# Output projection of the last two batches moved into the token-choice block, their router logits made from the product of both weights

## The chip, the cores and the metric

The kernel runs on one core of a Trainium2 chip. The metric is the time of one execution on the device, in microseconds (us).

## The reference, cut to what matters

Sixteen batches of 256 tokens with 256 features pass through a conditioned feed-forward layer (first block), then through a layer with attention of 16 heads of 64 and a mixture of 8 experts. What matters here is the end of attention and the choice of tokens:

```python
o = o.transpose(0, 2, 1, 3).reshape(b, n, H * HD)      # (tokens, 1024)
x = x + o @ Wout.T                                     # the output projection
tok = x.reshape(-1, d)                                 # 4096 x 256
gate = _softmax(tok @ Wgate.T, axis=-1)                # router logits, 8 experts
vals, idx = jax.lax.top_k(gate.T, k_cap)               # 512 tokens for each expert
...
g = _ln(tok[idx_flat], mlp_g, mlp_b)                   # gathered rows, normalised
...
tok = tok.at[idx_flat].add(y.reshape(-1, d))
```

## The kernel before

The program is three blocks with a barrier between them: `first_block`, `attention` and, in `experts`, a routing block followed by the expert block. Each engine has its own queue of instructions, written out in a fixed order, and waits on semaphores. An fp32 product is made of three products of high and low parts (`product`, line 147), so one 128-row tile of the output projection is 8 x 3 = 24 matmuls of 128x128 on 128x256.

**Attention** is one pipeline over steps t from -2 to 17, each of 8 head pairs s. In pair s of batch t TensorE does the scores of the pair (L1103), the transposes of the pair before (L1115) and the values of an older pair (L1130). VectorE takes the lowest score of each row (L1487), ScalarE the exponentials (L1258), and the scores of the next pair may start only when the exponentials have emptied the score banks. GpSimd divides (L1386). Into this pattern are put: parts of the next batches' q, k, v (`chunk`), "fills" on bank `tr` (`fill_at`: `h`, `qk`, and for the batch two steps back `x2`, the transposes of its new rows, L1201, and `gates`, its logits, L1206), and in pairs 2 and 3 the output projection of the batch before (`project`).

The last batch, 15, has no step after it. Its projection is done by head pair as `project_last` (L1154) in pairs 4 to 7 of step 15 and in `finish`; then VectorE adds the residual rows (`x2`, L1511), TensorE transposes them, ScalarE copies them, TensorE makes the logits and ScalarE puts them into `logit` (L1289). SyncE stores the new rows to `out` and the normalised rows to `x2_rows`.

**Routing.** After the barrier SyncE loads five small tables and then 8 MB of expert weights already split in halves (`load_halves`). VectorE and ScalarE make the softmax; TensorE transposes the gates (L1662). Then the 512th largest gate of every expert is found in 15 rounds ("digits"): VectorE counts against two trial values, ScalarE against a third with `Sign` (L1654), TensorE adds the counts (L1671), VectorE makes the next trial. TensorE fills the time with `idle_products` of the identity matrix (L1585), which nobody reads.

**Expert block.** GpSimd gathers rows from `x2_rows` by indirect DMA (L1971), TensorE transposes them (L1909), then two products for each expert, and GpSimd adds the results to `out`.

At the head of attention (t = -2 and -1) there are no scores yet. VectorE must first normalise the rows of batch 1, which SyncE loads after the barrier.

## Time and profile before

| what | value |
|---|---|
| median of 3 runs | 1431.27 us (1431.09 to 1432.25) |
| the profiled execution, time | 1431.61 us |
| its span, first to last instruction | 1429.8 us |
| TensorE busy | 1370.5 us, 96% |
| mean granted TensorE clock | 0.987 |

The profile lists each instruction or group with its start, duration, engine, source line and tiles ("out<-in"); in brackets stands the idle time ahead of it and what ended it. A TensorE row's duration overlaps the next row's: rates are read from the distance of starts. Granted clock 1.0 is 2.4 GHz, 0.5 is 1.2 GHz.

### The profile page before, as it was taken

What the parts mean: (1) busy time and instruction counts of PE and PEld (TensorE: products, weight loads), DVE (VectorE), ACT (ScalarE), POOL (GpSimd) and SP (SyncE); (2) the same over time, 40 slices, a digit from 0 to 9 for tenths busy, and PEclk for the clock granted to TensorE, in tenths of its full rate; (3) what the DMA queues carried; (4) which work ended last, traced back from release to release, by engine and by line L of the source; (5) the groups of instructions that cost most, each with busy time, mean ns of one, the idle gap of its engine ahead of it and who ended that gap; (6) DMA issues with size and microseconds to landing.
All of it is one profiled execution on the core that took longest, in us unless ns stands there. A gap on an engine that the chain in (4) does not pass through costs nothing. (4 is left out here: it accounts for less than half of the span.)

```text
span 1429.8 us, 30429 instructions
## 1 busy us (share of the span) xinstructions
PE 1370.5 (96%) x10795; PEld 1183.3 (83%) x10795; DVE 960.7 (67%) x2191; ACT 1035.9 (72%) x2703; POOL 911.5 (64%) x855
## 2 busy tenths in 40 slices
PE   7899999997899999999999999999999988999996
PEld 6799999996678887888888788788888777889896
DVE  5876667643776676677667667666755568678763
ACT  5556666565898889889888988988988732476662
POOL 2576666652678768867877876786787620354643
PEclk9899999999999999999999999999999999999999
DMA  5342222111100100110110011011011046145522
GB/s 159 114 129 67 68 67 68 49 45 30 38 9 30 53 23 31 53 45 9 52 46 31 30 53 36 18 53 45 9 45 46 30 148 253 45 104 156 137 35 30
DMA packets 61638, 89.04 MB, mean 62 GB/s; under 512 B 6144, under 2 KB 50992, under 8 KB 58800
## 3 DMA queue, kind: packets, MB, share of 16 engines
q1 hardware_dynamic: 53232, 75.82, 16.3%
q0 software_dynamic: 6144, 8.39, 3.6%
q10 hardware_dynamic: 2112, 2.88, 0.6%
q8 instruction: 87, 1.43, 0.4%
q14 instruction: 63, 0.52, 0.1%
HBM read 61.90 MB, written 25.18 MB: 61 GB/s over the span
## 5 line engine op out<-in xcount | busy, mean ns | idle before, releaser
L1386 POOL TENSOR_TENSOR prob<-prob,share_p 128x512 f32<-128x512 f32 x256 | 271.6, 1067 | 195.6 <-DVE share_p L1493 195.0
L1487 DVE TENSOR_REDUCE shift<-bank 128x2 f32<-128x512 f32 x256 | 164.7, 685 | 186.0 <-PE bank L1103 185.9
L1258 ACT ACTIVATE prob<-bank,shift 128x256 f32<-128x256 f32 x512 | 237.8, 479 | 64.3 <-DVE shift L1487 64.2
L147 PE MATMUL bank<-wqkv_h,rowsT_h 128*128 128x512 f32 x384 | 158.9, 414 | 2.8 <-PEq L311 1.7
L147 PE MATMUL bank<-wqkv_h,rowsT_l 128*128 128x512 f32 x384 | 151.5, 395 | 0.0
L147 PE MATMUL bank<-wqkv_l,rowsT_h 128*128 128x512 f32 x384 | 150.8, 393 | 0.0
L1115 PE MATMUL bank<-ident,prob 128*128 128x128 f32 x1024 | 142.7, 281 | 1.1 <-POOL prob L1386 1.1
L1374 POOL TENSOR_TENSOR landing<-landing,rq 128x512 f32<-128x512 f32 x128 | 131.1, 1046 | 8.4 <-DVE rq L1441 8.4
L1130 PE MATMUL bank<-pT,landing 128*64 128x256 f32 x1024 | 127.1, 388 | 1.7 <-ACT pT L1345 1.7
L1115 PEld LDWEIGHTS bank<-ident,prob 128*128 128x128 f32 x1024 | 109.5, 141 | 21.3 <-POOL prob L1386 3.7
L1258 ACT ACTIVATION_READ_ACCUMULATOR prob<-bank,shift 128x1 f32 x512 | 107.5, 210 | 0.0
L640 POOL TENSOR_TENSOR hid_l<-hid,hid_h 128x512 fp32r<-128x512 f32 x64 | 86.1, 1355 | 30.7 <-ACT hid_h L536 30.0
L1282 ACT ACTIVATE landing<-bank,cols 128x512 f32<-128x512 f32 x128 | 101.9, 796 | 4.9 <-PE bank L1196 3.3
L532 ACT ACTIVATE hid<-bank,cols 128x256 f32<-128x256 f32 x128 | 53.3, 470 | 68.0 <-PE bank L147 68.0
L1130 PEld LDWEIGHTS bank<-pT,landing 128*64 128x64 f32 x1024 | 67.5, 137 | 41.3 <-issue 9.8
L1103 PE MATMUL bank<-kT_h,qT_h 64*128 64x256 f32 x512 | 85.5, 329 | 2.7 <-ACT prob L1258 2.7
L1518 DVE COPY pT<-bank 128x512 f32<-128x512 f32 x128 | 87.2, 681 | 0.2 <-PE bank L1115 0.2
L1302 ACT ACTIVATE landing<-bank 128x512 f32<-128x512 f32 x128 | 80.2, 627 | 9.2 <-PE bank L147 9.1
L1483 DVE TENSOR_REDUCE ssq<-raw_sq 128x8 f32<-128x512 f32 x128 | 85.8, 673 | 1.3 <-ACT raw_sq L1304 0.8
L147 PEld LDWEIGHTS bank<-wqkv_h,rowsT_h 128*128 128x128 f32 x384 | 72.8, 190 | 16.3 <-issue 2.4
L1196 PE MATMUL bank<-ident,landing 128*128 128x128 f32 x512 | 78.2, 276 | 7.9 <-ACT landing L1282 3.7
L147 PEld LDWEIGHTS bank<-wqkv_h,rowsT_l 128*128 128x128 f32 x384 | 72.5, 189 | 15.8
(324 smaller groups left out, 4517.6 us busy)
## 6 DMA issues: line engine op xcount, KB each, us to landing
landing<-in_fc1s SPq DMA_DIRECT2D x6, 1024.0 KB
landing<-in_fc2s SPq DMA_DIRECT2D x6, 1024.0 KB
rows<-in_x SPq DMA_DIRECT2D x16, 256.0 KB, 2.9
xT<-in_xT SPq DMA_DIRECT2D x16, 256.0 KB, 2.7
x_again<-in_x SPq DMA_DIRECT2D x16, 256.0 KB, 2.8
x_rows<-x SPq DMA_DIRECT2D x16, 256.0 KB, 3.1
rows<-x_rows SPq DMA_DIRECT2D x16, 256.0 KB, 3.1
x<-x_rows SPq DMA_DIRECT2D x16, 256.0 KB, 2.9
```

The source lines that it names most:

```text
L147: last = nc.tensor.matmul(out, a, b, start=(n == 0), stop=(n == 3 * len(ks) - 1))
L640: nc.gpsimd.tensor_tensor(hid_l[:, 2 * g:2 * g + 2, :], hid[:, 2 * g:2 * g + 2, :], hid_h[:, 2 * g:2 * g + 2, :].bitcast(F32), ALU.subtrac ...
L1103: mm = nc.tensor.matmul(score_bank[side][:, n * T:(n + 1) * T], q[r, at, n * P:(n + 1) * P], k[r, at, :], start=(i == 0), stop=(i == 2))
L1115: last = nc.tensor.transpose(pT_bank[side][:, m * T + n * P:m * T + (n + 1) * P], prob[q % 2 * 2 + side][:, n, m * P:(m + 1) * P], ident[: ...
L1130: last = nc.tensor.matmul(values_bank(b, q)[side * HD:(side + 1) * HD, :], v[its][:, m, h * HD:(h + 1) * HD], pT[q % 2 * 2 + side][:, m, : ...
L1258: last = nc.scalar.activation(prob[at][:, n, :], score_bank[side][:, n * T:(n + 1) * T], ACT.Exp, bias=shift[:, at, n:n + 1], scale=-1.0, ...
L1282: nc.scalar.activation(raw_block(j), tr[:, :].rearrange("p (m n) -> p m n", m=4), ACT.Identity, bias=cols[:, g + 1:g + 2], scale=cols[:, g ...
L1374: nc.gpsimd.tensor_tensor(part, part, rq[:, n, c * 8:(c + 1) * 8].unsqueeze(2).to_broadcast([P, 8, HD]), ALU.mult).then_inc(normed, 1)
L1386: nc.gpsimd.tensor_tensor(prob[at][:, :, :], prob[at][:, :, :], share[:, at, :].unsqueeze(2).to_broadcast([P, TT, T]), ALU.mult).then_inc( ...
L1483: nc.vector.tensor_reduce(ssq[:, n, c * 8:(c + 1) * 8], raw_sq[c % 2][:, :].rearrange("p (h d) -> p h d", h=8), AX, ALU.add).then_inc(summ ...
L1487: nc.vector.tensor_reduce(shift[:, s % 2 * 2 + side, :], score_bank[side][:, :].rearrange("p (n m) -> p n m", n=TT), AX, ALU.min).then_inc ...
L1518: nc.vector.tensor_copy(pT[q % 2 * 2 + 1][:, :, :].rearrange("p m n -> p (m n)"), pT_bank[1][:, :]).then_inc(pT_dve, 1)
```

## The change

For the last `LATE` = 2 batches (14 and 15) attention no longer makes the projection. A matrix `wc`, Wgate times Wout (1024 x 8, in a high and a low part side by side, 16 columns), is made once at t = -1. `logits_of` multiplies it with the high and low parts of `o`: 16 matmuls with 256 moving columns for a batch. ScalarE copies the 16x256 result (`from_o`), and the `gates` fill adds it to the logits of the residual rows by one more small matmul for each 128 rows. The `x2` fill now transposes the residual rows themselves. `CLOSING_FILLS` says where these fills go.

The projection of both batches is done in the routing block: eight steps of three matmuls before the transposes of the gates, two steps in each of rounds 0 to 11 in place of the idle products. The rows of the batch are added by a matmul of the identity on `late_x`. ScalarE takes the result out, sums and squares it and normalises it between its `Sign` instructions, GpSimd makes the root. `o` of batch 14 is kept in DRAM meanwhile (`keep_o`), and is loaded into the place of the second early expert's first weights, which are loaded later.

The rows of batch 1 are loaded by SyncE in the last step of the first block. Buffers of `o`, `wout` and others share room with those of other blocks, and `ew_raw` becomes `ew_l`, so the next piece is loaded only when the store of the one before has landed.

```diff
+CLOSING_FILLS = {(NB - 1, 9): (NB - 2, "x2"), (NB - 1, 11): (NB - 2, "gates"), (NB - 1, 13): (NB - 1, "x2"), (NB, 3): (NB - 1, "gates")}
+LATE_PAIR = {False: PROJ_PAIRS[0], True: PROJ_PAIRS[1]}
...
@@ first_block, SyncE
+                    if at(t, NB):
+                        sp.wait_ge(tr_h, 1)
+                        sp.wait_ge(x1_out, 32)
+                        sp.dma_start(x_t[:, :, :], x1_rows[T:2 * T, :].rearrange("(t p) d -> p t d", p=P)).then_inc(x1_in, 16)
...
@@ attention, SyncE
+                    if t == -1:
+                        for q in range(4):
+                            sp.dma_start(prob[q][:, :, :], a["woutT"][:, q * T:(q + 1) * T].rearrange("(k p) n -> p k n", p=P)).then_inc(wc_in, 16)
...
+                    if is_late(t - 1) and live(t):
+                        keep_o(t - 1, (0, 2, 4, 6))
...
@@ attention, TensorE
+                def logit_weights():
+                    pe.wait_ge(wc_in, WC_IN + 64)
+                    for m in range(PAIRS):
+                        for k in range(KT):
+                            last = nc.tensor.matmul(score_bank[0][:, m * E:(m + 1) * E], prob[m // 2][:, k, m % 2 * P:(m % 2 + 1) * P], wgate[:, k, :],
+                                                    start=(k == 0), stop=(k == KT - 1))
+                    last.then_inc(wc_made, 1)
...
-                def project_last(k, its):
...
+                def logits_of(b, half, its):
+                    wait(pe, o_lo, PAIRS, b, 4 * half + 4)
...
+                    for k in range(4 * half, 4 * half + 4):
+                        for n, part in enumerate((o_h, o_l)):
+                            last = nc.tensor.matmul(chunk_bank[0][0:2 * E, 0:T], wc[:, k, :], part[:, o_at(k, its), :],
+                                                    start=(k == 0 and n == 0), stop=(k == PAIRS - 1 and n == 1))
...
                 def finish(t, its):
-                    fill(t, 1)
                     values(t - 1, PAIRS - 2, its)
                     transposes(t - 1, PAIRS - 1)
-                    project_last(PAIRS - 3, its)
+                    logits_of(t - 1, 0, its)
+                    values(t - 1, PAIRS - 1, its)
+                    logits_of(t - 1, 1, its)
                     fill(t, 3)
-                    values(t - 1, PAIRS - 1, its)
-                    project_last(PAIRS - 2, its)
-                    project_last(PAIRS - 1, its)
...
+                        if t == -1 and s == 2:
+                            logit_weights()
...
-                        if closing(t) and s in PROJ_PAIRS:
-                            project(t - 1, PROJ_PAIRS.index(s), 1 - odd)
-                        if closing(t) and s >= 4:
-                            for k in range(0 if s == 4 else s - 3, s - 2):
-                                project_last(k, odd)
                         if closing(t):
+                            if s == LATE_PAIR[True]:
+                                logits_of(t - 1, 0, 1 - odd)
+                                logits_of(t - 1, 1, 1 - odd)
                             fill(t, 2 * s + 1)
...
@@ routing block
+LATE_STEPS = [2] * 12 + [0] * 3
+TAKEN_IN, SPREAD_IN, NORMED_IN = {4: 1, 8: 2, 12: 3}, {5: 1, 9: 2, 13: 3}, {1: 0, 7: 1, 11: 2}
...
@@ routing, SyncE (after the five tables)
+                    for i, b in enumerate(LATE_ORDER):
+                        sp.dma_start(late_x[i][:, :, :], x1_rows[bass.ds(b * T, T), :].rearrange("(t p) d -> p t d", p=P)).then_inc(late_in[i], 16)
+                        if i > 0:
+                            load_late_o(i)
+                    load_halves(sp, w1_in, (w1_h, w1_l), halves[0:2], 0)
                     for e in range(EARLY):
-                        load_halves(sp, w1_in, (w1_h, w1_l), halves[0:2], e)
                         load_halves(sp, w2_in, (w2_h, w2_l), halves[2:4], e)
...
+                    for i, b in enumerate(LATE_ORDER):
+                        if i > 0:
+                            sp.wait_ge(late_made, NB + TT * (i + 1))
+                            load_halves(sp, w1_in, (w1_h, w1_l), halves[0:2], 1)
+                        sp.wait_ge(late_normed, NB + TT * (i + 1))
+                        for rows, tile, last in ((x2_rows, late_n[i], last_rows), (out, late_x[i], last_out)):
...
@@ routing, ScalarE
                     nc.scalar.activation(gates[:, :, :], gates[:, :, :], ACT.Exp).then_inc(exped, 1)
+                    take(0)
+                    spread_of(0)
                     for n in range(DIGITS):
...
@@ routing, TensorE
-                    idle_products(6)
+                    def late_step(i, k):
...
+                        if k == 0 and i % TT == 0 and j > 0:
+                            pe.wait_ge(late_in[j], 16 + 48)
+                        if k == HW // P - 1 and i == 0:
+                            pe.wait_ge(late_in[0], 16 + 16)
...
+                        for m, (o, w) in enumerate(((high, wo_h), (high, wo_l), (low, wo_h))):
+                            nc.tensor.matmul(late_bank(i), o[:, k, rows], w[:, k, :], start=(k == 0 and m == 0), stop=False)
+                        if k == HW // P - 1:
+                            nc.tensor.matmul(late_bank(i), ident[:, :], late_x[j][:, i % TT, :], start=False, stop=True).then_inc(late_made, 1)
+
+                    for k in range(HW // P):
+                        late_step(0, k)
+                    done = HW // P
                     pe.wait_ge(gated, 1)
...
-                    idle_products(6)
                     for n in range(DIGITS):
...
-                        idle_products(6)
+                        for _ in range(LATE_STEPS[n]):
+                            late_step(done // (HW // P), done % (HW // P))
+                            done += 1
+                        if LATE_STEPS[n] == 0:
+                            idle_products(6, 2, 384)
...
@@ expert block, GpSimd
+                        if first(later):
+                            pool.wait_ge(last_rows, 16 * (LATE_FROM + 1))
```

## Rows read from the trace of the kernel before

**Rows 1.** The page, busy time and share of TensorE.
```profile
PE 1370.5 (96%) x10795; PEld 1183.3 (83%) x10795; DVE 960.7 (67%) x2191; ACT 1035.9 (72%) x2703; POOL 911.5 (64%) x855
```

**Rows 2.** Timeline of TensorE, step 15: start us, us; scores, then one projection tile.
```profile
1126.44 0.39 PE L1103 MATMUL bank<-kT_h,qT_h 64*128 64x256 f32 x2
...
1132.44 0.38 PE L1103 MATMUL bank<-kT_h,qT_h 64*128 64x256 f32 x2
...
1135.39 0.39 PE L147 MATMUL bank<-wout_h,o_h 128*128 128x256 f32 x1
...
1138.24 0.28 PE L147 MATMUL bank<-wout_h,o_l 128*128 128x256 f32 x1
...
1150.71 0.39 PE L1103 MATMUL bank<-kT_h,qT_h 64*128 64x256 f32 x2
```

**Rows 3.** Timeline of TensorE, the tail after the last scores.
```profile
1155.04 1.08 PE L1130 MATMUL bank<-pT,landing 128*64 128x256 f32 x8
...
1156.90 0.36 PE L1154 MATMUL bank<-wout_h,o_h 128*128 128x256 f32 x1
...
1158.93 1.08 PE L1130 MATMUL bank<-pT,landing 128*64 128x256 f32 x8
...
1160.96 0.38 PE L1154 MATMUL bank<-wout_h,o_h 128*128 128x256 f32 x1
...
1164.97 1.03 PE L1206 MATMUL bank<-wgate,proj 128*128 128x8 f32 x8 [0.78 <-ACT proj L1286]
```

**Rows 4.** Timeline of ScalarE and VectorE in the same stretch.
```profile
1129.90 0.21 ACT L1258 ACTIVATION_READ_ACCUMULATOR prob<-bank,shift 128x1 f32 x1
...
1162.72 0.76 DVE L1511 TENSOR_TENSOR x<-bank,x 128x256 f32<-128x256 f32 x2 [1.82 <-DMA x<-x_rows]
...
1166.04 0.18 ACT L1289 ACTIVATE logit<-bank 128x16 f32<-128x16 f32 x1 [1.21 <-PE bank L1206]
```

**Rows 5.** Timeline of SyncE's queue in the routing block.
```profile
1167.08 0.35 SPq L1635 DMA_DIRECT2D tables<-in_tables  x1
...
1169.45 0.36 SPq L1589 DMA_DIRECT2D ew_h<-split_w1h  x1
...
1195.50 0.33 SPq L1595 DMA_DIRECT2D landing<-in_fc2s  x1
```

**Rows 6.** The tile `x_rows`: from issue to landing, all its transfers.
```profile
DMA to landing us min/median/max: 2.1/3.0/5.3
```

**Rows 7.** Timeline of the routing block: gates, first and last round.
```profile
1170.21 0.44 PE L1662 MATMUL bank<-ident,gates 128*128 128x128 f32 x2 [0.18 <-DVE gates L1713]
...
1171.54 0.51 ACT L1654 ACTIVATE signs<-key,trial 128x256 bf16<-128x256 f32 x1 [2.68 <-DVE key L1720]
...
1198.96 0.51 ACT L1654 ACTIVATE signs<-key,trial 128x256 bf16<-128x256 f32 x1 [1.30 <-DVE trial L1764]
```

**Rows 8.** Groups by line: a squaring pass of ScalarE with a sum.
```profile
L540 ACT ACTIVATE junk_act<-rows 128x256 f32<-128x256 f32 x32 | 12.9, 405 | 1.5 <-DMA rows<-in_x 1.5
```

**Rows 9.** Timeline at the head of attention.
```profile
330.62 0.75 DVE L1446 BATCH_NORM_STATS2 stats<-rows 128x6 f32<-128x256 f32 x2 [3.60 <-DMA rows<-x_rows]
...
334.68 0.50 PE L147 MATMUL bank<-wqkv_h,rowsT_h 128*128 128x512 f32 x1 [0.82 <-ACT raw_sq L1304]
...
341.55 0.66 PE L1196 MATMUL bank<-ident,landing 128*128 128x128 f32 x4 [0.63 <-POOL landing L1374]
...
342.97 0.81 ACT L1282 ACTIVATE landing<-bank,cols 128x512 f32<-128x512 f32 x1
```

**Rows 10.** Window 1218:1220 us: busy by engine, PEclk, DMA share, GB/s.
```profile
1218.00:1220.00 2.00, 1.00 (x12) 0.55 (x11) 0.00 (x0) 0.00 (x0) 1.04 (x2) 0.50 0.22 70
```

**Rows 11.** Timeline of the expert block's start: the same small matmul twice, the first gather.
```profile
1211.35 0.29 PE L1902 MATMUL bank<-rec,spread 128*128 128x48 f32 x1 [0.33 <-DVE rec L2022]
...
1212.98 2.14 POOL L1971 DMA_INDIRECT gx<-x_rows,next_index  x1 [0.18 <-POOL idle L1958]
...
1220.40 0.41 PE L1902 MATMUL bank<-rec,spread 128*128 128x48 f32 x1 [0.30 <-DVE rec L2022]
```

More of the change, by code:

```diff
@@ L926, in fill_at, with attention @@
             slot += 1
-        if slot == i:
+        if slot == i and not (name in ("x2", "gates") and t + TR_LAG[name] >= NB - 2):
             return t + TR_LAG[name], name, j
     return -1, None, 0
-def attention(nc, exponent, weights, rows_of, banks, ident, x1_rows, hbias, cols, x2_rows, logit, out, a, halves, sbuf, sems):
+def attention(nc, exponent, weights, rows_of, banks, ident, x1_rows, hbias, cols, x2_rows, logit, out, a, halves, out_weights, o_kept, o_stored,
+              spent, sbuf, sems):
+    wo_h, wo_l, o_h, o_l, _ = out_weights
+    wc_in, wc_made, wc_done = spent
     landing, o_raw, wgate, wo_hi, wo_lo, (x2_stored, x2n_stored, ew_stored) = weights
@@ L1543, in step @@
                             chains(t, i + 1, spot)
+                        if t == -1 and s == 2:
+                            logit_weights()
                         for j in range(8):
@@ L1558, in _, with experts @@
                 steps(step)
-def experts(nc, a, landing, halves, banks, ident, cols, x2_rows, logit, out, stored, sbuf, sems):
+LATE_STEPS = [2] * 12 + [0] * 3
+TAKEN_IN, SPREAD_IN, NORMED_IN = {4: 1, 8: 2, 12: 3}, {5: 1, 9: 2, 13: 3}, {1: 0, 7: 1, 11: 2}
+def experts(nc, a, exponent, landing, halves, banks, ident, cols, x1_rows, x2_rows, logit, out, stored, out_weights, o_kept, o_stored,
+            spent, sbuf, sems):
+    late_stored, late_made, late_taken, late_centred, late_squared, late_normed, late_rooted, late_links, *late_in = spent
+    wo_h, wo_l, o_h, o_l, kept = out_weights
     s = ExitStack()
@@ new lines, in _ @@
+                    sp.wait_ge(late_stored, LATE_STORED + 32 * (LATE - 1))
+                @block.gpsimd
+                def _(pool):
+                    link = Links(pool, late_links)
+                    link.base = NB
+                    for i in range(LATE * TT):
+                        one = slice(i, i + 1)
+                        pool.wait_ge(late_squared, NB + i + 1)
+                        link(nc.gpsimd.tensor_scalar(late_var[:, one], late_sq[:, one], 1.0 / D, LN_EPS, ALU.mult, ALU.add))
+                        link(nc.gpsimd.tensor_tensor(late_root[:, one], late_var[:, one], exponent[:, :], ALU.pow))
+                        nc.gpsimd.tensor_tensor(late_shift[:, one], late_mean[:, one], late_root[:, one], ALU.mult).then_inc(late_rooted, 1)
```

271 lines of the change are left out of this document (177 added, 94 removed).

## The prediction

> **What bounds the kernel now.** I read the page first: TensorE is busy for 96% of the span [rows 1], so a matmul taken away counts where TensorE is what ends last, and nowhere else. The last step of attention and the routing block are the places touched, so I read their timelines next, engine by engine.
>
> In step 15 a head pair without additions is 2.95 us of TensorE work (scores 1132.44, first projection matmul 1135.39). A projection tile adds 24 matmuls between 1135.39 and 1138.24, which is 0.12 us each and about 3.06 us with the change of operands: pair 2 lasts 6.00 us [rows 2]. But there is a second loop under it. The last exponential of pair 2 is read out at 1129.90 + 0.21 = 1130.11, 3.67 us after its scores began [rows 2, 4], and the next scores may not start before. So a pair can't be shorter than about 3.75 us, however little TensorE has to do. The reader is to see that 0.8 us of each bare pair is not TensorE's.
>
> After the last scores the tail is a chain: values of pair 7 at 1158.93, the last part of the projection at 1160.96, the new rows on VectorE only at 1162.72 because their residual came by a late DMA, logits at 1164.97, `logit` written at 1166.04 [rows 3, 4]. The routing block starts at 1167.08 [rows 5]. In it the chain is gates transposed (1170.21), first `Sign` (1171.54), and 14 steps of (1198.96 - 1171.54) / 14 = 1.96 us to the last one [rows 7]. TensorE's idle products there cost nothing: this stretch is a chain through all engines, and it is where the moved work goes.
>
> **The change part by part: steps 15 and 16.** I move through it with the starts before as clock.
> - Pair 2 loses its tile and falls on the floor: 3.75 for 6.00 us, -2.25.
> - Pairs 3 to 6 took 1150.71 - 1132.44 = 18.27 us [rows 2]. After: pair 3 with 16 matmuls of `logits_of`, 2.95 + 16 x 0.12 + 0.2 = 5.05; pair 4 with the `x2` fill, four transposes at 0.23, 3.87; pair 5 with the `gates` fill, 8 small matmuls in 1.03 [rows 3] and two more of the same kind, 0.25, 4.2; pair 6 with the other `x2` fill, 3.87. Sum 16.99, -1.28. That a 16-column stationary tile streams like one of 128 is my assumption; the moving side has the same 256 columns.
> - Pair 7 to the values of pair 6: 4.33 us before (1155.04), bound by ScalarE's copy of the transposed tile after the exponentials; 4.2 after, -0.13.
> - From 1155.04 the values and transposes are as before until 1156.90 [rows 3]; then 8 matmuls of `logits_of` (1.15 us, to 1158.05) for the work that held the values of pair 7 back to 1158.93: -0.88. Running sum -4.5.
> - The tail: values to the last projection part was 1160.96 - 1158.93 = 2.03. After it: 8 matmuls and their latency 1.1, ScalarE's copy of 16x256 with its semaphores 0.5, the gates fill 1.07 to the start of the `logit` copy [rows 3, 4] plus 0.25. The `logit` copy starts 2.03 + 1.1 + 0.5 + 1.32 = 4.95 us after the values; before it was 1166.04 - 1158.93 = 7.11: -2.16. The late residual DMA, its add, the transposes and the copy leave the path.
>
> Sum -6.7. If pair lengths are 0.15 over my floor and the small copies cost 0.5 more it is -5.9; if the barrier, which last followed SyncE's store, comes faster, -7.3.
>
> SyncE is moved past too: the eight stores of `keep_o`, the 2 waits for landing in `load_piece`, the residual loads of batches 14 and 15. They are issued pairs before their readers; batch 14's rows are wanted only at the end of pair 4. Covered, 0; without the cover each would cost its landing, median 3.0 [rows 6].
>
> **Routing: what waits first.** Eight late steps are put ahead of the gate transposes on TensorE. 21 of their matmuls run at once, but the last three wait for `late_x[0]`, which SyncE issues after the five tables. The sixth transfer of this block was issued at 1169.45 [rows 5]; a read or write of `x_rows` lands 3.0 us after issue in the median, 2.1 at least, 5.3 at most [rows 6]. So the rows are there at 1172.45, and behind them in TensorE's order stand three matmuls (0.46 with the start), the identity matmul on 256 fp32 columns (0.24, twice a 128-column one) and then the transposes of the gates, at about 1173.2 for 1170.21 [rows 7]: +3.0. ScalarE has `take(0)` and `spread_of(0)` ahead of its first `Sign`: 0.41 each [rows 8], 0.2 each for reading the sum [rows 4] and a small one between, some 1.4 us from 1173.3, to 1174.7. VectorE has the key at 1174.5. `Sign` is thus 0.2 late, and VectorE's two counts, longer, hide it. I take +3.0; bounds by the landings +2.1 and +5.3.
>
> In the rounds two late steps are 6 x 0.12 = 0.7 us against a round of 1.96, after the sum of counts and not ahead of it; 0. ScalarE's extra passes (at most 1.4 us behind a `Sign` of 0.7) leave nothing over in rounds 5, 9 and 13 but do fit by about 0.2; a miss costs a few tenths. GpSimd is free here. `o` of batch 14 is wanted in round 4, some 8 us after the first; fine.
>
> **Head of attention.** VectorE no longer waits 3.60 us for the rows of batch 1 [rows 9]; its sums then come earlier and TensorE's wait of 0.82 goes. But `logit_weights` puts 16 small matmuls, twice the 1.03 us of the gates fill [rows 3], at the place where TensorE idled 0.63 before the first `qk` fill at 341.55 [rows 9]. After: last chunk ends 0.9 earlier, 2.0 us of these, fill at 342.05. ScalarE empties the fill at 342.97, held by its own queue [rows 9]; that queue is up to 0.9 ahead, the fill's data 0.5 late and ready at 342.7: -0.2 in all. Bounds: -0.9 (all of the early rows) and +0.6 (none of it, the products in full).
>
> **Sum.** -6.7 + 3.0 - 0.2 = -3.9. The profiled execution took 1431.61, 0.34 over the median, at 1429.8 of span; I apply the difference to the median: 1431.27 - 3.9 = 1427.4 us.
>
> **The rivals.** (1) *The full gain*, if the rows of batch 15 are not waited for: 24 matmuls from 1167.13 end at 1170.0, when the gates are ready anyway. Then +0.2 for +3.0: 1424.6. The three last matmuls would want the rows at 1169.7, with an issue at 1169.45 [rows 5]; rows 6 show no landing under 2.1. So it is left only as a landing at the minimum together with more from the tail or the head: 0.07.
>
> (2) *The clock.* TensorE now stands about 3 us before the gates and has 6 matmuls for 12 idle products in a round. Where it had stood about half of the time, the clock granted was 0.50 [rows 10], and the same small matmul took 0.41 for 0.29 us [rows 11]. If the rounds run at 1.2 GHz, each has 0.12 more on its chain: 15 x 0.12 = +1.8, 1429.2. Against it: 6 x 256 columns are as many as 12 x 128. 0.15. The Trainium skill ("TensorE: Matmul & The Clock Gate", "HAM oscillation") has the same warning, that gaps between bursts of matmuls bring the lower clock back; it speaks against taking the filler out, and by it the sum would be rival 2's. Rows 10 agree that a sparse stretch loses the clock; whether this one does, none shows.
>
> (3) *Slower: the gather waits for rows.* GpSimd's first gather (1212.98 before, about 1216 by the clock above) now waits until batch 14's `x2_rows` have landed. They are stored after the last late norm, near 1203, behind the second fc2 megabyte (issued 1195.50 before [rows 5]), the b2 rows, and 2 MB of `w1` halves. At 9 MB in the 26 us from 1169.45 to 1195.50 these 4.5 MB take 13 us, to about 1210. It decides from 1216 on; the kernel is slower by 0.2% only with a landing 6.8 us later still, 1223. Price at 1225: +9 - 3.9 = +5, 1436. 0.07.
>
> (4) *The pairs don't shrink*: the gain of steps 15 and 16 is only that of the tail, -3.0, and the sum is 0: 1431.2. Speaks for it: five engines share the loop. Against: TensorE's rows are back to back there. 0.05.
>
> **How the numbers follow.** The forecast has 0.66. Within 0.2% is +-2.9 us, about what a measurement can tell. The forecast's own range is 1425.5 to 1429.2 (tail -7.3 to -5.9, landing, head). The range 1424.0 to 1430.2 takes in rivals 1 and 2. Faster by over 0.2%, below 1428.4: most of the forecast (0.58), rival 1 (0.07), a third of rival 2 (0.05): 0.70. Slower: rival 3 and overruns of landings, 0.08. The rest, 0.22, is the same.
>
> **What would show it.** Right: step 15's scores at pair 3 start 3.75 us after those of pair 2; the `logit` copy of batch 15 near 1159.4 and the barrier near 1160.4; TensorE then idle for some 3 us up to a DMA wait, the gates transposed 6.1 us after the block's first DMA (3.1 before); 15 rounds of 1.96. Wrong: a gate transposition at 3.3 us (rival 1), PEclk of 0.5 in the rounds (2), an idle GpSimd before the first gather with a DMA as releaser (3), pairs of 5 us (4). I would also be wrong if a 16-column product streamed slower, or the sums on ScalarE stretched rounds 5, 9 and 13.

## The result and the profile after

| | median, us | lowest to highest | profiled execution, its span | mean granted clock |
|---|---|---|---|---|
| before | 1431.12 | 1429.31 to 1434.29 (20 runs) | 1431.61, 1429.8 | 0.987 |
| after | 1432.99 | 1430.89 to 1438.23 (20 runs) | 1433.03, 1431.2 | 0.981 |

The ratio after to before is 1.0019, 95% interval 1.0012 to 1.0026: 1.9 us slower (0.13%), inside the 0.2% that I called the same, and 5.6 us above the forecast of 1427.4. The range of 1424.0 to 1430.2 doesn't hold it.

The two profiles differ by 1.4 us, measured to the start of the last matmul. Cut at events that both have, the difference lies here (from the timelines; B is the routing block's first instruction on TensorE):

| stretch | before | after | difference | predicted |
|---|---|---|---|---|
| start to attention's first matmul | 328.00 | 328.17 | +0.2 | 0 |
| to the first `logit` copy (head) | 145.57 | 147.55 | +2.0 | -0.2 |
| to the 13th `logit` copy (12 full steps) | 609.21 | 610.06 | +0.9 | 0 |
| to B (steps 15 and 16) | 84.35 | 78.29 | -6.1 | -6.7 |
| B to the first `Sign` | 4.41 | 8.65 | +4.2 | +3.0 |
| first to last `Sign` | 27.42 | 28.68 | +1.3 | 0 |
| to the last matmul | 219.79 | 218.71 | -1.1 | 0 |
| sum | | | +1.4 | -3.9 |

So most of the gain is there (how much of it is the change's own is worked out in the section on why the prediction was wrong), and five other stretches together cost more than it. TensorE's row of the page, for [rows 1], gives no hint of that; it is 3.7 us less busy in a longer span:

```profile
PE 1366.8 (95%) x10707; PEld 1177.7 (82%) x10707; DVE 956.1 (67%) x2178; ACT 1043.8 (73%) x2727; POOL 913.2 (64%) x864
```

**Step 15** (answers to [rows 2]). Timeline of TensorE, first scores of pairs 2 to 7:

```profile
1128.84 0.39 PE L1147 MATMUL bank<-kT_h,qT_h 64*128 64x256 f32 x2
...
1132.56 0.38 PE L1147 MATMUL bank<-kT_h,qT_h 64*128 64x256 f32 x2 [0.71 <-ACT prob L1306]
...
1138.20 0.39 PE L1147 MATMUL bank<-kT_h,qT_h 64*128 64x256 f32 x2
...
1141.93 0.39 PE L1147 MATMUL bank<-kT_h,qT_h 64*128 64x256 f32 x2
...
1146.65 0.39 PE L1147 MATMUL bank<-kT_h,qT_h 64*128 64x256 f32 x2
...
1150.38 0.39 PE L1147 MATMUL bank<-kT_h,qT_h 64*128 64x256 f32 x2
```

Pair 2 is 3.72 us, and TensorE stands 0.71 there for the last exponential: the floor that I had worked out at 3.75. The pair with a `x2` fill is 3.73 (3.87 predicted). The pair with the additions of `logits_of` is 5.64 (5.05), the one with the `gates` fill 4.72 (4.2). Pairs 3 to 6 together are 17.82 us, for 16.99 predicted and 18.27 before.

The tail (answers to [rows 3, 4]), timeline of TensorE and ScalarE:

```profile
1159.59 1.11 PE L1196 MATMUL bank<-kept,wc 128*16 128x256 f32 x8 [0.94 <-DVE kept L1575]
...
1163.58 0.18 ACT L1339 ACTIVATE logit<-bank 128x16 f32<-128x16 f32 x1 [2.42 <-PE bank L1254]
```

The values of pair 7 start at 1157.56, so the `logit` copy follows them by 6.02 us: 4.95 was predicted, 7.11 was before.

The 16-column product streams like a 128-column one (8 records in 1.11 us), so that assumption held.

**Head of attention** (answers to [rows 9]), timeline of TensorE, then ScalarE:

```profile
339.86 3.97 PE L1130 MATMUL bank<-wgate,prob 128*128 128x8 f32 x32
343.68 1.09 PE L1241 MATMUL bank<-ident,landing 128*128 128x128 f32 x4
...
344.82 0.78 ACT L1330 ACTIVATE landing<-bank,cols 128x512 f32<-128x512 f32 x1 [2.60 <-PE bank L1241]
```

`logit_weights` is 16 matmuls in the code, and 32 records and 3.97 us in the trace. I had priced it at 2.0, from the fill of [rows 3], whose "x8" are the records of 4 matmuls and not 8 matmuls. ScalarE, which had been behind [rows 9], now waits 2.60 us for TensorE.

**Routing** (answers to [rows 5, 7]), timeline of TensorE, SyncE and ScalarE:

```profile
1164.08 4.82 PE L1814 MATMUL bank<-kept 128*128 128x256 f32 x21 [0.53 <-PEq L1064]
1164.15 0.33 SPq L1726 DMA_DIRECT2D tables<-in_tables  x1
...
1167.55 0.43 SPq L1732 DMA_DIRECT2D late_x<-x_rows  x1
...
1170.39 0.62 PE L1814 MATMUL bank<-kept 128*128 128x256 f32 x3 [1.49 <-DMA late_x<-x_rows]
...
1171.28 0.38 PE L1823 MATMUL bank<-ident,gates 128*128 128x128 f32 x2
...
1172.73 0.49 ACT L1792 ACTIVATE signs<-key,trial 128x256 bf16<-128x256 f32 x1
...
1174.30 1.63 PE L1814 MATMUL bank<-kept 128*128 128x256 f32 x6
```

The order is the predicted one: 21 late matmuls, a stand for the rows of batch 15, three more, the identity, the gates, and ScalarE's `take` and `spread_of` before the first `Sign`. Two things are not. The rows are issued 3.4 us after the block's first transfer (2.4 assumed; one table's issue took 1.56). And the 21 matmuls took 4.82 us, 0.23 each where the same kind takes 0.12 in [rows 2]: in 1164:1168 the granted clock is 0.50, half of it. Six such matmuls in a round took 1.63 us, and with the count sum before them they fill 2.0 us, so that TensorE sets the pace. The rounds of the two kernels, from one `Sign` to the next (us):

| | 1 | 2 | 3 | 4 | 5 | 6 | 7 | 8 | 9 | 10 | 11 | 12 | 13 | 14 |
|---|---|---|---|---|---|---|---|---|---|---|---|---|---|---|
| before | 2.15 | 1.90 | 1.90 | 1.90 | 1.90 | 1.91 | 2.42 | 1.90 | 1.90 | 1.91 | 1.90 | 1.90 | 1.90 | 1.90 |
| after | 2.18 | 2.01 | 2.00 | 2.00 | 2.59 | 1.93 | 2.42 | 1.90 | 2.12 | 1.93 | 1.90 | 1.90 | 1.90 | 1.90 |

Windows over the rounds, before and after (us, then busy time and instructions of TensorE, its weight loads, VectorE, ScalarE, GpSimd; granted clock; DMA share and GB/s):

```profile
1172.00:1180.00 8.00, 7.15 (x56) 6.58 (x57) 7.01 (x39) 2.55 (x10) 0.00 (x0) 1.00 1.01 423
1180.00:1188.00 8.00, 7.18 (x57) 6.42 (x56) 6.90 (x42) 2.27 (x9) 0.00 (x0) 1.00 1.01 418
```

```profile
1172.00:1180.00 8.00, 6.36 (x26) 5.70 (x26) 6.77 (x35) 3.57 (x12) 0.93 (x3) 0.53 1.00 407
1180.00:1188.00 8.00, 6.13 (x34) 5.34 (x34) 6.30 (x37) 3.12 (x12) 0.94 (x3) 0.83 1.01 426
1188.00:1196.00 8.00, 6.45 (x34) 5.53 (x34) 6.75 (x37) 4.20 (x15) 0.92 (x3) 0.79 0.77 317
```

The sixth number, after POOL's, is the granted clock: 1.00 before, 0.53, 0.83 and 0.79 after. The busy times look alike, because at half the clock the same work keeps TensorE busy for longer; the instruction counts are the thing to read, 56 against 26 in the first window. At the full clock six late matmuls are 0.96 us of TensorE, and the 12 records of idle products that they replace were 1.58.

### The profile page after: what moved, and what is told of

Read it like the earlier page. It is cut to its first block and busy times, and to the rows that moved or that the text cites. A ratio compares the mean times of both kernels' runs of the same rounds, so it can differ in the third digit from the quotient of the medians.

```text
span 1431.2 us, 30291 instructions
## 1 busy us (share of the span) xinstructions
PE 1366.8 (95%) x10707; PEld 1177.7 (82%) x10707; DVE 956.1 (67%) x2178; ACT 1043.8 (73%) x2727; POOL 913.2 (64%) x864
## 5 line engine op out<-in xcount | busy, mean ns | idle before, releaser
L147 PE MATMUL bank<-kept 128*128 128x256 f32 x1440 | 183.1, 285 | 0.0
L147 PEld LDWEIGHTS bank<-kept 128*128 128x128 f32 x1440 | 175.3, 191 | 0.0
L656 POOL TENSOR_TENSOR kept<-hid,kept 128x512 fp32r<-128x512 f32 x64 | 86.4, 1360 | 31.1 <-ACT kept L552 30.5
L147 PE MATMUL bank<-kept,w_h 128*128 128x256 f32 x512 | 95.8, 287 | 0.0
L147 PE MATMUL bank<-ew_h,kept 128*128 128x256 f32 x512 | 94.2, 283 | 0.0
```

Source lines behind the costliest of these rows:

```text
L147: last = nc.tensor.matmul(out, a, b, start=(n == 0), stop=(n == 3 * len(ks) - 1))
L656: nc.gpsimd.tensor_tensor(hid_l[:, 2 * g:2 * g + 2, :], hid[:, 2 * g:2 * g + 2, :], hid_h[:, 2 * g:2 * g + 2, :].bitcast(F32), ALU.subtrac ...
```

## The experiments

Each is made from the changed kernel unless said otherwise. The kernel before ran beside them on the same chip (medians 1430.9 for the first four, 1431.1 for the next four, 1430.88 for the three after and 1432.58 for the last), and ratios are to it. In code cuts `...` stands for lines left out.

### The head, the late rows, the idle products

**One eighth of the products of wc.**

```diff
-                    for m in range(PAIRS):
+                    for m in range(1):
```

> Of the eight groups of wc = wo x wg in the head only the first is made (2 of its 16 matmuls), and its result is copied into all eight, so the logits of the last two batches are not the reference's; nothing else is left out. Theory (the products lie on the path: 32 records, 3.97 us, in the changed kernel's trace, and everything behind stands about 2.1 us later): the kernel is 1.7 to 2.3 us faster than the changed one, near 1430.9, and the first qk fill of the head starts near 341.6 instead of 343.7. Rival (the head is late because the clock granted there is 0.50, and the products only fill a gap): less than 0.5 us, 1432.6 to 1433.0. Second rival (the products cost, but ScalarE's queue holds the next wait, as I reckoned before): 0.5 to 1 us.

Measured: 1433.82 us, ratio 1.0018 (1.0010 to 1.0027).

**Products of wc in four lots.**

```diff
+                        if t == -1 and s in (4, 5, 6):
+                            logit_weights(range(2 * s - 6, 2 * s - 4))
                         fill(t, 2 * s)
...
-                        if t == -1 and s == 2:
-                            logit_weights()
+                        if t == -1 and s == 3:
+                            logit_weights(range(0, 2))
```

> All products of wc are made, but in four lots of 4 matmuls ahead of four qk fills (in pairs 3 to 6 of the head) instead of 16 in one place. Theory (the cost of the 16 is that they stand together where TensorE has no slack, and where there is slack later, as TensorE waits for a bank behind ScalarE, a lot of 1 us hides): 1 to 2 us faster than the changed kernel, 1431 to 1432. Rival (TensorE sets the pace of every pair of the head, so work is work): no difference, 1432.7 to 1433.3.

Measured: 1431.31 us, ratio 1.0001 (0.9992 to 1.0009). By whole times this is a contradiction: taking the products away gains nothing, spreading them 1.7 us. The stages settle it. From the last `Sign` on, the run with one eighth takes 221.0 us for 218.7; its logits choose other tokens, so that its whole time can't be compared. And the head depends on the clock it happens to be granted. All profiled executions of the study, head (attention's first matmul to the first `logit` copy) against the mean granted clock in 340:400:

| kernel | 0.94 | 0.91 | 0.89 |
|---|---|---|---|
| before, and before with fewer idle products | 145.57 | 147.25 | |
| products in one place (after and four variants) | 145.85, 145.90, 145.92 | 147.51, 147.55 | |
| one eighth of the products | | 146.35 | |
| four lots (five variants) | 144.67, 144.69 | 146.10, 146.25, 146.45 | |
| products in one place, batch 1's rows late | | | 149.84 |

Within a column each kind lies within 0.35 us. One step of the clock costs 1.65 us, whatever the kernel. At the same clock the changed head costs +0.3 over before, the 16 products in one place 1.2 over none, and in four lots they cost nothing. What is left against before, -0.9 in one column and -1.0 in the other, I put down to the early load; the direct test of it further down did not settle it. So the theory on the products holds, at 1.2 us and not at 2 (read from one execution with one eighth of them and from five with the four lots); of the profile's +2.0 us, 1.7 was the clock that this execution was granted.

**Rows of batch 15 ahead of the tables.**

```diff
+                    sp.dma_start(late_x[0][:, :, :], x1_rows[...]).then_inc(late_in[0], 16)
                     for t, src in ((tables[:, :], a["tables"]), ...
```

> SyncE issues the load of batch 15's rows before the five tables of the routing block and not behind them. Theory (the start of the routing block is bound by the landing of these rows, issued 3.4 us after the first of the block's transfers): they land 3 us sooner, the gates are transposed about 1.5 us sooner (then the 21 matmuls of the late steps at half clock, ending 4.8 us after the block's first, are next), the kernel 1 to 2 us faster, 1431 to 1432. Rival (the late matmuls at half clock bind already, and the landing is hidden): under 0.3 us. Second rival (the tables, then late, become what the first Sign waits for): no gain or a loss of up to 1 us, with a wait of ScalarE or VectorE for a DMA.

Measured: 1432.23 us, ratio 1.0009 (1.0001 to 1.0018). Timeline of TensorE, its late matmuls and the gates:

```profile
1163.59 3.78 PE L1815 MATMUL bank<-kept 128*128 128x256 f32 x21 [0.53 <-PEq L1064]
1168.23 1.01 PE L1815 MATMUL bank<-kept 128*128 128x256 f32 x3 [0.85 <-DMA late_x<-x_rows]
1169.03 1.05 PE L1817 MATMUL bank<-late_x,ident 128*128 128x256 f32 x2
1169.88 0.63 PE L1824 MATMUL bank<-ident,gates 128*128 128x128 f32 x2
```

The gates come 6.29 us after B for 7.20, less than the 1.5 expected, since TensorE still gets the rows 4.6 us after their issue at 1163.66 and the matmuls behind them run at half clock. B to the first `Sign` is 7.82 for 8.65. The rounds took 30.86 us in this execution, with the clock between 0.50 and 0.67 in three windows of 8 us: the small gain of the start can be lost in them.

**Six idle products back behind the gates.** Their line (`idle_products(6, 2, 384)`) was put back where the kernel before has it.

> The changed kernel with the six products on idle operands put back behind the transposes of the gates, where the kernel before had them. Theory (the clock of 0.50 in the first rounds comes from the 2 us in which TensorE then has nothing, and at it six late matmuls take 1.63 us, so that rounds last 2.0 to 2.6 us instead of 1.9): the granted clock rises sooner, first to last Sign takes 27.4 to 27.9 for 28.68 us, the kernel 0.7 to 1.2 us faster, 1431.8 to 1432.3. Rival (the low clock comes from the stand before the rows land, and six products more cannot mend it): within 0.3 us, and the rounds keep 28.7. Second rival (the products stand ahead of the count sum and delay it): slower by up to 0.7 us.

Measured: 1433.42 us, ratio 1.0020 (1.0009 to 1.0030): no gain. Windows over the rounds:

```profile
1172.00:1180.00 8.00, 5.25 (x37) 4.34 (x35) 7.00 (x37) 3.19 (x11) 0.93 (x3) 1.00 1.00 412
1180.00:1188.00 8.00, 5.62 (x31) 4.63 (x30) 6.80 (x42) 3.81 (x15) 0.94 (x3) 0.80 1.01 424
```

They only move the fall: the clock is 1.00 in the first rounds, which hold 5.25 us of TensorE in 8, and then falls inside the rounds, where nothing had been put back. First to last `Sign` is 28.18 us. That the fall came from the missing six alone, which was my theory, is refuted. All twelve runs lie between 1431.3 and 1438.9 us with mean clocks of 0.985 down to 0.974, the longest at the lowest.

### What decides the clock in the rounds

**Idle products in each round**, beside those behind the gates:

```diff
-                        if LATE_STEPS[n] == 0:
-                            idle_products(6, 2, 384)
+                        idle_products(6 if LATE_STEPS[n] == 0 else 3, 2, 384)
```

> The changed kernel with three products on idle operands in each round that has late steps (six more records, some 0.75 us of TensorE at 2.4 GHz, behind the six late matmuls) and six behind the transposes of the gates. Theory (a late step's six matmuls take 0.96 us at the high clock where the kernel before had 12 records of idle products in 1.58 us; TensorE is then busy 1.2 to 1.35 us in each 2 us instead of 1.93, the granted clock falls to 0.50, and at that clock TensorE is the longest of the round): the granted clock stays at 1.00 through the rounds, first to last Sign takes 27.4 to 27.9 us, the kernel 0.6 to 1.4 us faster than the changed one, 1431.4 to 1432.3. Rival (the clock goes by something else, for instance the stand at the rows of batch 15, or the late matmuls cost ScalarE and VectorE their slots): rounds of 28.2 or more with the clock at 1.00. Second rival (once the clock falls, a fuller round at 0.50 is longer still): rounds over 30 us, slower than the changed kernel by 1 us or more.

Measured: 1432.59 us, ratio 1.0009 (1.0000 to 1.0018). Windows over the rounds:

```profile
1172.00:1180.00 8.00, 7.91 (x61) 7.28 (x62) 7.05 (x36) 3.37 (x11) 0.20 (x2) 1.00 0.99 410
1180.00:1188.00 8.00, 7.41 (x58) 6.78 (x57) 6.80 (x41) 3.93 (x14) 0.99 (x3) 1.00 1.01 421
1188.00:1196.00 8.00, 7.90 (x63) 7.27 (x61) 6.82 (x36) 4.19 (x16) 0.93 (x3) 1.00 0.60 250
```

The clock stays at 1.00 throughout, and first to last `Sign` is 27.67 us for 28.68: the mechanism is as supposed. The whole time shows less of it, 0.4 us in the medians with intervals that overlap. In the profile 0.65 us of the 1.0 is lost again right behind the rounds, where VectorE stands 1.42 us at the routing block's end for 0.77 in the changed kernel; the last group of experiments says for what.

**The kernel before with half of its idle products**, the same question asked without any of the change:

```diff
-                        idle_products(6)
+                        idle_products(3)
```

> The kernel before with three idle products in each of its 15 rounds instead of six, nothing else changed: six records of 0.12 us where the changed kernel has six late matmuls of 0.16. Theory (TensorE's busy share in the rounds decides the clock there): the granted clock falls to 0.50 in part of the rounds, first to last Sign takes 27.9 to 29.5 us for 27.42, the kernel is 0.5 to 2 us slower than before. Rival (the stand at the rows of batch 15 and the late steps' waits bring the clock down, not the share in the rounds): the clock stays at 1.00, and the time is that of before within 0.3 us, or a little less, as TensorE is done earlier in each round.

Measured: 1435.51 us, ratio 1.0026 (1.0018 to 1.0035): taking work from TensorE makes the kernel before slower, by 4.4 us between the medians and 3.7 by the ratio, more than expected. Windows over the rounds, then TensorE in one round and behind the rounds:

```profile
1172.00:1180.00 8.00, 5.86 (x39) 5.07 (x39) 6.74 (x35) 2.40 (x8) 0.00 (x0) 0.92 0.97 362
1180.00:1188.00 8.00, 7.83 (x33) 7.09 (x32) 6.69 (x40) 1.98 (x7) 0.00 (x0) 0.50 1.01 424
1188.00:1196.00 8.00, 7.55 (x32) 6.59 (x32) 6.62 (x37) 2.40 (x9) 0.00 (x0) 0.50 0.96 398
```

```profile
1184.69 1.63 PE L1585 MATMUL bank<-ident 128*128 128x128 f32 x6
...
1206.94 4.06 PE L1585 MATMUL bank<-ident 128*128 128x128 f32 x24
```

The rounds take 28.48 us for 27.42, and the last `Sign` to the expert block 9.47 for 7.35, because the half clock outlives the rounds and the 24 records of idle products at the block's end are then in the way. These two stages explain 3.2 us. This is the clean proof that the filler was not free to take away; the prediction had said that it costs nothing, which holds only as long as it stays. The Trainium skill ("TensorE: Matmul & The Clock Gate", "HAM oscillation") warns that gaps between bursts of matmuls bring the lower clock back; the gap it describes is a wait for DMA. The trace agrees with the direction of that rule: here the clock falls at 1178.75 us with no wait for DMA, after rounds in which TensorE stands 0.74 us at a time for VectorE.

**Rows first, late steps split around the gates, idle products in the rounds:**

```diff
-                    for k in range(HW // P):
+                    for k in range(4):
                         late_step(0, k)
-                    done = HW // P
                     pe.wait_ge(gated, 1)
...
                     last.then_inc(tr_gates, 1)
+                    for k in range(4, HW // P):
+                        late_step(0, k)
+                    done = HW // P
```

> Rows of batch 15 loaded ahead of the five tables, only four late steps ahead of the transposes of the gates and four behind them (ScalarE's first take and spread move into the first two rounds), and three idle products in each round with late steps. Theory (the routing start is bound by what stands ahead of the gates on TensorE and by the landing): routing's first TensorE instruction to the first Sign takes 4.4 to 5.5 us instead of 8.65, the rounds 27.4 to 28.4 with the clock at 1.00, in sum 3 to 4.5 us faster than the changed kernel, 1428.5 to 1430. Rival (the half clock that the tail of attention leaves behind makes the first four late steps as late as the eight): the first Sign at 6.5 us or more, 1430.5 to 1431.5.

Measured: 1430.83 us, ratio 0.9999 (0.9991 to 1.0008). Timeline of TensorE and ScalarE:

```profile
1163.95 2.90 PE L1813 MATMUL bank<-kept 128*128 128x256 f32 x12 [0.53 <-PEq L1064]
...
1167.04 0.69 PE L1821 MATMUL bank<-ident,gates 128*128 128x128 f32 x2 [0.18 <-DVE gates L1877]
...
1168.62 0.51 ACT L1791 ACTIVATE signs<-key,trial 128x256 bf16<-128x256 f32 x1 [2.94 <-DVE key L1884]
```

B to the first `Sign` is 4.67 us for 8.65; the gates wait for VectorE again, as before the change, and the half clock of the 12 matmuls is hidden. Against the run with filler alone the stage is 3.7 us shorter (8.40 there) and the medians differ by 1.8 us (1432.59 to 1430.83), with intervals that overlap a little; the wait at the block's end has grown from 1.42 to 2.08 us.

**The same with the products in four lots**, both edits together.

> The same as the run with four late steps ahead of the gates and idle products in the rounds, and the products of wc in four lots in the head. Theory (the head's lots hide, as the run with them alone was 1.7 us below the changed kernel in the median): 1 to 1.8 us under the run without them, 1427 to 1429, which is under both kernels. Rival (what the run with the lots gained was the clock's chance in the head, since without any products nothing was gained): no difference to the run without them.

Measured: 1428.3 us, ratio 0.9981 (0.9973 to 0.9990): faster than both kernels, by intervals that exclude 1. The lots are worth 2.5 us in these medians, of which the head's 1.2 is sure and the rest is not explained. The wait at the block's end is 3.10 us in this execution.

### The early rows, the price of the filler, the last wait

**The early load of batch 1's rows undone.**

```diff
-                    if at(t, NB):
-                        sp.wait_ge(tr_h, 1)
-                        sp.wait_ge(x1_out, 32)
-                        sp.dma_start(x_t[:, :, :], x1_rows[T:2 * T, :]...).then_inc(x1_in, 16)
...
-                    if live(b) and b > 1:
+                    if live(b):
```

> The changed kernel with one part undone: batch 1's rows are loaded where the kernel before loads them, in attention's own first step, and not in the first block's last one. Theory (in the traces so far the head of attention, from its first matmul to the first logit copy, is 145.6 us before, 145.9 after and 144.7 with the products in four lots, each read where the granted clock falls for the shorter time; so the early rows give 0.9 and the products in one place cost 1.2): the head is 0.7 to 1.0 us longer than the changed kernel's, read at the same granted clock, and the kernel 0.5 to 1 us slower than the changed one. Rival (the products stand where VectorE's wait for the rows would be anyway, so the two cover each other): the head is the same within 0.3 us.

Measured: 1433.06 us, ratio 1.0021 (1.0012 to 1.0030), beside 1.0019 for the changed kernel. VectorE waits 3.65 us for the rows again, but the execution had a clock of 0.89 in 340:400, which no other had. Taking the 1.65 us of one step off leaves 148.2 for 147.5, an estimate of 0.7 for the early rows. The direct test is thus inconclusive: the whole times are equal, and the head could not be read at an equal clock. What the early rows give is shown only by the -0.9 and -1.0 of the table above, where it is what remains after the products.

**Without the idle products in the three rounds with an identity matmul** (numbers 3, 7 and 11, counted from 0).

```diff
-                        idle_products(6 if LATE_STEPS[n] == 0 else 3, 2, 384)
+                        idle_products(6 if LATE_STEPS[n] == 0 else 0 if n % 4 == 3 else 3, 2, 384)
```

> The best version so far (rows first, four late steps ahead of the gates, idle products in the rounds, wc in four lots) without the idle products in the three rounds in which a late tile is closed by its identity matmul, since such a round then holds some 2.5 us of TensorE against a pace of 1.9. Theory: each of the three is 0.2 to 0.5 us shorter and the clock stays up, as the neighbours are full: 0.5 to 1.2 us faster than that version, 1427 to 1428. Rival (one emptier round lets the clock fall): the rounds run at 0.50 in part, 0.5 to 2 us slower than it. Second rival: no difference.

**Without idle products in any round with late steps**: that line as in the changed kernel.

> The same version with no idle products in the rounds with late steps at all, to price them alone. Theory (the clock falls in the rounds without them): first to last Sign 28.5 to 31 us, 1 to 2.5 us slower than that version, 1429.3 to 1431. Rival (the split of the late steps already keeps TensorE going at the start, and the clock holds in the rounds): within 0.4 us of it.

Measured: trimmed 1428.59 us, ratio 0.9980 (0.9971 to 0.9990); none 1427.90, ratio 0.9976 (0.9967 to 0.9985). Neither differs from the full filler's 0.9981, so both forecasts missed: the trimming gained nothing that shows, and the filler as a whole neither. In the profiles the rounds are as the theory says: 27.47 us for 28.29 with the trimmed filler (0.4 of it is the first round, 2.16 for 2.57, the rest some 0.14 in each of the three), all rounds from the second on within 0.02 of before's; 28.84 without filler, with a clock of 0.64 and 0.72 in the last two windows of 8 us. But the version without it is no slower. In the two profiles the reason is behind the rounds. The trimmed kernel, VectorE and SyncE's queue, with the landing of `late_n`:

```profile
1195.47 0.43 SPq L1753 DMA_DIRECT2D x_rows<-late_n  x1
1195.94 0.48 SPq L1753 DMA_DIRECT2D out<-late_x  x1
...
1204.45 1.22 DVE L2172 TENSOR_TENSOR in_row<-slot_low,steps 128x1024 f32<-128x1024 int32 x1 [1.78 <-PEq L1721]
```

```profile
DMA to landing us min/median/max: 7.9/7.9/7.9
```

The block can't end before batch 15's rows are stored. SyncE issues the two stores at 1195.47 and 1195.94, behind 1 MB loads; the first lands at 1203.4, the second at 1204.0, and the barrier opens 0.5 later. VectorE stands 1.78 us at it, for 0.78 before. Last `Sign` to expert block is 8.36 us trimmed, 7.35 without filler: of the 1.4 us that the rounds gain, this wait takes 1.0. In the changed kernel it was hidden behind slower rounds (7.34). It also is what stood at the block's end in the three runs with full filler (1.42, 2.08 and 3.10 us): there too the barrier opens 0.45 us after the second store has landed.

**The stores of batch 15 ahead of the fc2 weights:**

```diff
                     load_raw(sp, w1_raw, a["fc1s"], EARLY, 0, 0)
+                    store_late(0)
                     load_raw(sp, w2_raw, a["fc2s"], EARLY, 0, 1)
```

> The trimmed version with one more edit: SyncE issues the two stores of batch 15's rows as soon as they are normed, ahead of the raw second-layer weights of expert 2, and not 1.5 us behind their issue. Theory (the rounds at the full clock gain 1.3 us, but the version with them is no faster than the one without, because SyncE's last wait of the routing block, for these stores issued at 1195.47 and landed 7.9 us later, then holds the barrier: VectorE stands 1.78 us there for 0.77 in the kernels whose rounds are longer): VectorE's wait at the barrier is back at 0.8 us, last Sign to the expert block's first instruction 7.3 us for 8.36, the kernel 0.7 to 1.1 us faster than the trimmed one, 1427.2 to 1428.0. Rival (something else of the block ends at the same time, such as the last norm's store): the barrier stays within 0.3 us and so does the time. Second rival (the gather or the first weights wait in the expert block anyway, so that the barrier's microsecond is given back before fc1): the barrier moves, fc1 and the end don't.

Measured: 1428.49 us, the kernel before 1432.58 beside it, ratio 0.9970 (0.9959 to 0.9981). The barrier moved as the theory says:

```profile
1183.59 0.37 SPq L1739 DMA_DIRECT2D x_rows<-late_n  x1
...
1203.12 1.23 DVE L2177 TENSOR_TENSOR in_row<-slot_low,steps 128x1024 f32<-128x1024 int32 x1 [0.77 <-PEq L1721]
```

Last `Sign` to expert block is 7.34 us. The best ratio of the study, but its interval overlaps that of the two versions before it, so the microsecond is shown at the barrier and not in the whole time. Two other stages of this execution are longer than in the trimmed one. From the expert block's start to fc1 it took 19.41 us for 18.80, which is the second rival in part. And its first round took 3.42 us for 2.16, which the moved stores don't explain: the granted clock is 0.50 in 1166:1170, the four late steps behind the gates take 2.91 us for 2.03, and VectorE waits for the sum of counts behind them:

```profile
1169.87 0.16 DVE L1926 SCALAR_TENSOR_TENSOR passed<-bank,trial 128x4 f32<-128x4 f32 x1 [1.43 <-PE bank L1840]
```

So the split is not free either: the late steps behind the gates stand ahead of the first count sum, and the first round took 2.16, 2.23, 2.52, 2.57 and 3.42 us in the five executions that have it, for 2.15 before.

## Why the prediction was wrong

The profile missed the sum by 5.3 us (+1.4 for -3.9). By stage that is +2.2 in the head, +1.3 in the rounds, +1.2 in the routing start, +0.9 in the twelve full steps, +0.6 in steps 15 and 16, +0.2 at the start, and -1.1 after the rounds.

**Steps 15 and 16, -6.7: right mechanism, a little too large, and closer in the profile than it should be.** Measured -6.1, but the clock helped. Windows of the stretch just before step 15's second pair, before and after:

```profile
1083.00:1127.00 44.00, 41.05 (x336) 32.39 (x336) 25.22 (x58) 35.71 (x104) 35.60 (x34) 0.96 0.11 37
1086.00:1129.00 43.00, 39.47 (x330) 31.22 (x330) 25.20 (x58) 35.57 (x104) 35.76 (x34) 1.00 0.23 75
```

The profile of the kernel before has a part at the lower clock there; from the 13th to the 14th `logit` copy it takes 44.02 us, and 43.15 in the same code with fewer idle products. That one needs 83.33 us for steps 15 and 16, and the four executions made from the change that keep a clock of 1.00 need 77.72 to 77.76: a gain of 5.6. The floor of a pair, the streaming of the 16-column product and the earlier values of pair 7 came out. Pairs 3 to 6 were 0.8 longer than their terms: 0.6 too much in the one with `logits_of`, 0.5 in the one with the `gates` fill, a little less in the other two. Values to `logit` copy took 6.02 us for 4.95, and there it is the `gates` fill again: from its first matmul to the copy it is 2.3 us here, and 1.8 in the run with one eighth of the products, whose clock is 1.00, for 1.32 in my term. A barrier 0.6 us closer to the `logit` copy, which I had counted only in the range, gave some of it back.

**"I take +3.0" for the routing start: right mechanism, too small.** Measured +4.2, inside the bounds of +2.1 to +5.3. Of the 1.2 us, 1.0 is the issue of the rows (3.4 us after the block's first DMA for 2.4). The split run shows what the order costs: 8.65 against 4.67.

**"In the rounds ...; 0": wrong, and this was the failed step of reasoning.** I priced the late steps at the high clock, said that the idle products cost nothing, and set rival 2 at 0.15 with "6 x 256 columns are as many as 12 x 128". Equal columns are not equal time: 12 records of the fp32 product are 1.58 us of TensorE, six late matmuls 0.96. What the runs show in place of the 0: the granted clock falls (0.77 on average from first to last `Sign`, for 1.00), and the rounds take 28.68 us for 27.42; with filler back the clock stays at 1.00 and they take 27.67. The rival was right in kind. Its price of +1.8 is near the +1.3 here, but that is luck, since its mechanism (0.12 on each small matmul) is not the one: at the half clock the six late matmuls take 1.63 us and TensorE itself becomes the round. How dear the fall can be, the kernel before with fewer idle products shows.

**Head, -0.2: right size at equal clock, wrong terms.** The profile's +2.0 is 1.7 of clock, which no term had. At equal clock the stretch is +0.3 (bounds -0.9 to +0.6). The products were priced at 2.0 and took 3.97, of which 1.2 lay on the path; what is left for the early rows is 0.9, all of what they could give by my bound.

**Not in my sum at all:** the 12 full steps between, +0.9 in the profile. All but the last, which is 0.4 us shorter everywhere, were 50.80 us each in the profiles of the kernel before and of its variant with fewer idle products, and 50.82 to 50.89 in those made from the change, with the same matmuls back to back. In six of those steps the matmuls with `wqkv_l` as weights stand 33.01 us for 32.90, those with `rowsT_l` moving 33.89 for 33.79: half of the 0.4 us that these six steps differ by. Where that comes from was not tried, and it stays open; that buffers lie elsewhere is one candidate, argued and not shown.

**Rivals.** Rival 3, the gather behind batch 14's rows, did not come: last `Sign` to the last matmul is 1.1 us shorter, not longer. Rival 4 is refuted by the pairs, rival 1 by the DMA wait at 1170.39.

Together, with the head and steps 15 and 16 at equal clocks: +0.2 +0.3 +0.9 -5.6 +4.2 +1.3 -1.1 = +0.2 for the profile. The median of +1.9 has the half clock falling more often and for longer. First to last `Sign` suggests it: 28.7, 30.2, 30.9 and 30.9 us in the four variants that leave these rounds as they are. So do the 20 runs of the changed kernel: the six with a mean granted clock of 0.974 to 0.978 took 1433.0 to 1438.2 us, the six with 0.982 or 0.983 took 1430.9 to 1432.4, while no run of the kernel before whose clock is on record is under 0.983. Where in these runs the clock fell is not known, so that the fall lies in the rounds stays an inference from single profiles. A single profile is a weak scale for less than 2 us in any case: the stretch before attention's first matmul took 327.9 to 330.5 us in the fourteen of this study.

## What to carry to other kernels

When real matmuls take the place of idle ones, compare how long each kind keeps TensorE busy (here 0.96 us for 1.58), and not their number or columns. If the stretch gets emptier, look at its granted clock: here it fell, and real work that had been hidden became the pace. Moving work out of a TensorE-bound stage into a latency-bound chain gains little if the work stands ahead of the chain's own first step: four late steps instead of eight in front of the gates, and their rows loaded first, shortened that stage by 4 us (8.65 to 4.67), of which the medians show some 2, since a wait behind it grew. And once a chain is shortened, look for the next wait at the barrier behind it, here a store queued behind megabytes of weights.

## What the hardware showed that I had not expected

- A product of fp32 operands shows as two records, and a record with 8 moving columns costs nearly as much as one with 128 or, for the late matmuls, 256: 0.124 us (32 in 3.97), 0.13 (12 in 1.58) and 0.16 (6 in 0.96). Each of these holds the last one's end once; from start to start they are 0.11, 0.11 and 0.12 us within a group.
- The head of attention comes in steps 1.65 us apart (145.57 and 147.25 for the same code), each with 0.028 less of mean clock over 60 us. A difference of less than that between two profiles can be the clock's; the same stage at the same granted clock repeated within 0.35 us.
- Idle products at the half clock are not idle: 24 records take 4.06 us for 2.84 and hold the next block back.
